# Scores of a lightning-attention layer from 96-row stacks of q and k halves, filled by transfers, instead of one zero-padded fp32 matmul a group

## The reference

```python
x = x + layernorm(attention(layernorm(x)))
x = x + layernorm(moe(layernorm(x)) + sigmoid(x @ shared_gate.T) * shared_ffn(layernorm(x)))

# attention: 16 heads of 32, chunks of 128 tokens, state S (32x32 a head) over a sequence
inter  = (q * decay_q) @ S
scores = (q @ k.T) * dmask            # 128 x 128 a head and chunk
intra  = scores @ v
S      = lam_c * S + (k * decay_k).T @ v
out    = inter + intra
```

## Time and profile before

| | |
|---|---|
| median of 3 runs | 1981.48 us (1980.39 to 1983.88) |
| the profiled execution | 1979.72 us, of which the span is 1977.9 |
| PE busy | 1883.4 us, 95% |
| DVE, ACT, POOL busy | 1084.6, 844.1, 437.3 us |
| transfers | 456.84 MB, 231 GB/s |

### The profile page before, as it was taken

How to read it: one execution, slowest core, us unless ns; L and a number is a source line. 1 busy time by engine, 2 the same in 40 slices (tenths; PEclk the granted TensorE clock), 3 DMA queues, 4 the chain that set the end, 5 groups by cost and what they waited for, 6 DMA issues and landing times.

```text
span 1977.9 us, 27565 instructions
## 1 busy us (share of the span) xinstructions
PE 1883.4 (95%) x9880; PEld 1530.1 (77%) x9880; DVE 1084.6 (55%) x2590; ACT 844.1 (43%) x1718; POOL 437.3 (22%) x438
## 2 busy tenths in 40 slices
PE   7779999999999998999999999989999999999997
PEld 5566777777777776777777777868899999999875
DVE  4556664564464463354464454353566667666566
ACT  4334443333343333333244233112566666666554
POOL 2301001001002000100100100120355656655322
PEclk9899999999999999999999999999999999999998
DMA  8978566646466446536556546687688999889597
GB/s 294 373 267 306 176 241 237 238 160 240 164 224 234 163 169 249 200 126 235 191 204 235 178 133 256 240 306 279 209 239 261 281 273 273 253 261 267 123 281 201
DMA packets 140869, 456.84 MB, mean 231 GB/s; under 512 B 17200, under 2 KB 17344, under 8 KB 123968
## 3 DMA queue, kind: packets, MB, share of 16 engines
q1 hardware_dynamic: 90720, 251.70, 36.3%
q0 software_dynamic: 49584, 203.33, 33.2%
q10 hardware_dynamic: 432, 0.07, 0.0%
HBM read 332.99 MB, written 122.04 MB: 230 GB/s over the span
## 4 chain that ended last, share of the span: by engine, by line
PE 63%; DVE 5%; DMA 1%; ACT 1%; issue 1%; SPq 0%; ACTq 0%; POOL 0%; DVEq 0%
PE banks L797 18%; PE banks L799 18%; PE banks L798 18%; PE banks L864 2%; PE banks L990 2%; PE banks L996 1%; PE banks L878 1%; PE banks L884 1%; PE banks L871 1%; DMA att_w_lo<-att_w_split 1%; PE banks L830 1%; DMA ffn_w_raw<-w_ffn 1%; DVE fin_stats L1536 0%; DVE probsT L1361 0%; PE banks L860 0%
## 5 line engine op out<-in xcount | busy, mean ns | idle before, releaser
L797 PE MATMUL banks<-xT_hi,ffn_gate_up_hi_lo 128*128 128x512 f32 x704 | 296.2, 421 | 10.1 <-DMA xT_lo<-xt_scratch 3.0
L799 PE MATMUL banks<-xT_hi,ffn_gate_up_hi_lo 128*128 128x512 f32 x704 | 276.2, 392 | 0.0
L798 PE MATMUL banks<-xT_lo,ffn_gate_up_hi_lo 128*128 128x512 f32 x704 | 275.1, 391 | 0.0
L797 PE MATMUL banks<-moe_gu_hi,moe_xT_hi 128*128 128x352 f32 x568 | 195.8, 345 | 0.3 <-DVE moe_xT_lo L1516 0.3
L1068 ACT COPY q_one_head<-qT 32x128 f32<-32x128 f32 x512 | 151.2, 295 | 88.6 <-PE banks L864 83.1
L799 PE MATMUL banks<-moe_gu_hi,moe_xT_lo 128*128 128x352 f32 x568 | 183.5, 323 | 0.0
L1509 DVE TENSOR_TENSOR moe_gu_lo<-moe_gu_raw,moe_gu_hi 128x704 fp32r<-128x704 f32 x156 | 136.3, 890 | 85.4 <-ACT moe_gu_hi L1129 77.0
L798 PE MATMUL banks<-moe_gu_lo,moe_xT_hi 128*128 128x352 f32 x568 | 182.4, 321 | 0.0
L797 PEld LDWEIGHTS banks<-xT_hi,ffn_gate_up_hi_lo 128*128 128x128 f32 x704 | 132.5, 188 | 50.2 <-issue 13.9
L683 POOL DMA_INDIRECT ffn_out<-moe_y,moe_x x71 | 123.6, 1741 | 159.0 <-DMA ffn_out<-moe_y,moe_x 40.6
L798 PEld LDWEIGHTS banks<-xT_lo,ffn_gate_up_hi_lo 128*128 128x128 f32 x704 | 132.7, 188 | 33.6 <-issue 8.9
(11 more groups left out here) (318 smaller groups left out, 4155.4 us busy)
## 6 DMA issues: line engine op xcount, KB each, us to landing
ffn_gate_up_hi_lo<-ffn_gate_up_split SPq DMA_DIRECT2D x66, 1024.0 KB
ffn_down_hi_lo<-ffn_down_split SPq DMA_DIRECT2D x66, 512.0 KB, 3.6
att_w_hi<-att_w_split SPq DMA_DIRECT2D x112, 256.0 KB, 4.0
att_w_lo<-att_w_split SPq DMA_DIRECT2D x112, 256.0 KB, 5.0
x_normed_by_expert<-x_normed POOLq DMA_DIRECT2D x26, 771.0 KB, 16.0
ffn_w_raw<-w_ffn SPq DMA_DIRECT2D x44, 384.0 KB, 6.3
ffn_gate_up_split<-ffn_gate_up_hi_lo SPq DMA_DIRECT2D x11, 1024.0 KB, 3.9
x_in<-x SPq DMA_DIRECT2D x32, 256.0 KB, 3.7
```

The source lines that it names most:

```text
L797: pe.matmul(out_ap, l_hi, r_hi, start=start, stop=False)
L798: pe.matmul(out_ap, l_hi, r_lo, start=False, stop=False)
L799: return pe.matmul(out_ap, l_lo, r_hi, start=False, stop=stop)
```

## The change

For blocks 1 to 7 the scores are made in another way. ACT copies q and k of a chunk, all four groups, rounded to fp32r (hi), and DVE subtracts them (lo): the new piece SQ, into `qk_parts`. SP then issues 12 transfers for each half of the groups, the new piece sx: for each of 4 heads of a group three 32-row bands, so that a stack of 96 rows holds q hi, q hi, q lo on one side and k hi, k lo, k hi on the other. The stacks lie in the memory of x_normedT (`qk_stack`). S is then four fp32r matmuls, 96 rows deep, 128 by 128, one for each head. Block 0 still has Z and the fp32 matmul. q_decayed now lies in qT itself for blocks 1 to 7. All the places of `PLACES` and `OPENING` are drawn anew, `PASSES` counts 2 for S, and in the expert stage the pieces XT and HT stand one place earlier.

```diff
 PLACES = {
...
-    "QK": (9.66, 11.07, 12.07, 13.22, 14.07, 15.07, 16.07, 16.78,),
+    "QK": (10.86, 11.47, 11.78, 11.8, 11.88, 12.85, 14.89, 15.52,),
...
+    "SQ": (17.03, 28.94, 33.88, 39.38,),
+    "sx": (23.79, 27.2, 27.41, 28.52, 33.14, 35.7, 42.92, 45.63,),
+    "KT": (25.54, 31.56, 37.12, 46.82,),
+    "S": (27.14, 27.84, 30.05, 30.38, 32.72, 33.54, 34.57, 35.31, 38.59, 39.3, 42.57, 43.12, 44.96, 47.22, 48.88, 49.38,),
...
@@ moe_step
-    split()
     if j + 1 < NJ:
         out += [("XT", j + 1)]
+    split()
+    if 1 <= j <= NJ:
+        out += [("HT", j - 1)]
     if live:
         out += [("GU", j, 1)]
     split()
-    if 1 <= j <= NJ:
-        out += [("HT", j - 1)]
...
+        xa = sb("x_normedT_hi_lo", [2, KT, TOK], F32R, scope=phase1)
+        xa_hi, xa_lo = xa[:, 0], xa[:, 1]
+        qk_stack = xa[:, :, :, :].rearrange("p s k t -> p (s k t)").rearrange("p (h s j g t) -> p h s j g t", h=2, s=2, j=GH, g=G // 2)
...
+        qk_parts = sb("qk_hi_lo", [2, 2, G, P], F32R, scope=phase1)
+        qz = qk_parts[:, 0].bitcast(F32)
...
+        def q_decayed(a, c):
+
+            return qT[:, :, c * P:(c + 1) * P] if a else first_qd
+
+        def stacked(a, c):
+
+            return 16 * 3 * GH * (NC * (a - 1) + c)
...
+            elif kind == "sx":
+                a, c, h = args
+                sp.wait_ge(v_piece, done("V", "SQ", a, c))
+                if c == 0:
+                    sp.wait_ge(p_piece, max(done("P", "V", a, NC - 1), done("P", "QK", a, 2 * G - 1)))
+                else:
+                    sp.wait_ge(p_piece, done("P", "S", a, c - 1, 2 * h + 1))
+                for r, (q_part, k_part) in enumerate(((0, 0), (0, 1), (1, 0))):
+                    for j in range(GH):
+                        src = qk_parts[j * HD:(j + 1) * HD, :, :, 2 * h:2 * h + 2, :].rearrange("p s i g t -> p (s i) (g t)")
+                        first, step = q_part, 2 + k_part - q_part
+                        sp.dma_start(out=qk_stack[r * HD:(r + 1) * HD, h, :, j].rearrange("p s g t -> p s (g t)").bitcast(F32),
+                                     in_=src[:, first:first + step + 1:step, :].bitcast(F32)).then_inc(stack_in[h], 16)
...
             elif kind == "S":
                 c, g = args
-                pe.wait_ge(a_piece, done("A", "Z", a, c, g))
-                mm = pe.matmul(b, kT[:, g, c * P:(c + 1) * P], qz[:, g % 2].rearrange("p h t -> p (h t)"),
-                               start=True, stop=True)
+                h, gl = divmod(g, 2)
+                pe.wait_ge(stack_in[h], stacked(a, c + 1))
+                for j in range(GH):
+                    mm = pe.matmul(b[:, j * P:(j + 1) * P], qk_stack[0:3 * HD, h, 1, j, gl, :], qk_stack[0:3 * HD, h, 0, j, gl, :],
+                                   start=True, stop=True)
...
+            elif kind == "SQ":
+                c, = args
+                if (a, c) == (1, 0):
+                    act.wait_ge(p_piece, done("P", "S", 0, NC - 1, G - 1))
+                if c == 0:
+                    act.wait_ge(a_piece, done("A", "QK", a, 2 * G - 1))
+                if (a, c) > (1, 0):
+                    for h in range(2):
+                        act.wait_ge(stack_in[h], stacked(a, c))
+                op = act.copy(qk_parts[:, :, 0], qkT[:, :, :, c * P:(c + 1) * P])
...
+                if a:
+                    ve.wait_ge(a_piece, done("A", "SQ", a, c))
+                    ve.wait_ge(v_piece, done("V", "SQ", a, c))
+                ve.tensor_tensor(q_decayed(a, c), qT[:, :, c * P:(c + 1) * P], dq[:, :, :], ALU.mult)
...
+            elif kind == "SQ":
+                c, = args
+                ve.wait_ge(a_piece, done("A", *piece))
+                op = ve.tensor_tensor(qk_parts[:, :, 1], qkT[:, :, :, c * P:(c + 1) * P], qk_parts[:, :, 0].bitcast(F32),
+                                      ALU.subtract)
```

More of the change, by code:

```diff
@@ L88 @@
[L88 to L110, removed]
+    "xin": (-26.98, -25.61, -25.39, -23.54,),
+    "N1A": (1.79,),
+    "N1B": (3.89,),
+    "N1": (4.54, 5.75, 7.57, 7.72,),
+    "T1": (5.87, 7.74, 8.2, 8.53,),
+    "wa": (5.47, 6.48, 8.73, 9.2, 11.13, 11.62, 12.83, 15.03, 14.9, 16.86, 17.56, 17.65, 25.58, 25.35, 23.26, 23.39,),
@@ new lines @@
+    "ST": (31.14, 36.38, 44.24, 53.74,),
+    "OUT": (32.88, 36.66, 44.63, 52,),
+    "LO": (37.13, 52.58,),
+    "LN": (40.01, 54.09,),
+    "L": (40.74, 55.29,),
+    "LX": (42.44, 56.85,),
+    "x1o": (40.59, 42.18, 54.75, 57.86,),
+    "T2": (43.87, 46.29, 59.01, 59.17,),
+    "xto": (61.05,),
+    "R1": (60.3,),
+    "R2": (63.97,),
+    "SM1": (64.06,),
+    "SM2": (64.16,),
+    "SM3": (64.51,),
+    "SM4": (66.38,),
+    "CM": (65.6,),
+    "RK": (68.51,),
+    "sc": (62.14,),
+    "PG": (69.92,),
@@ L122 @@
     "T1": (4.47, 5.52, 6.47, 6.59,),
[7 rows of a table removed]
-    "OUT": (28.96, 35.39, 44.8, 50.87,),
[9 rows of a table added]
+    "OUT": (29.04, 34.37, 46.23, 50.88,),
 }
-ARGS = {"Z": (NC, G), "S": (NC, G), "IP": (NC, 2)}
+ARGS = {"Z": (NC, G), "sx": (NC, 2), "S": (NC, G), "IP": (NC, 2)}
 def attention_offsets(a):
@@ L266, in final_chunk @@
     return [("FX", q), ("fo", q)]
-PASSES = {"T1": 2, "QK": 12, "V": 12, "KT": 2, "S": 4, "IP": 6, "ST": 4, "OUT": 12, "T2": 2, "R1": 12, "R2": 2, "RK": 1,
+PASSES = {"T1": 2, "QK": 12, "V": 12, "KT": 2, "S": 2, "IP": 6, "ST": 4, "OUT": 12, "T2": 2, "R1": 12, "R2": 2, "RK": 1,
           "GA": 12, "UP": 12, "DN": 12}
@@ L574, in build @@
         xt_used = sem("xT_used")
+        stack_in = [sem(f"qk_stack_in{h}") for h in range(2)]
         xs_zero, acc_zero, unused_id = sem("x1_by_expert_zero"), sem("ffn_out_zero"), sem("unused_row_id")
@@ L860, in pe_attention @@
                     mm = pe.transpose(b[:, g * P:(g + 1) * P], kT[:, g, c * P:(c + 1) * P], ident[:, :])
+            elif kind == "S" and a == 0:
+                c, g = args
+                pe.wait_ge(a_piece, done("A", "Z", a, c, g))
+                if c == 0:
+                    pe.wait_ge(a_piece, done("A", "QK", a, G + g))
+                mm = pe.matmul(b, kT[:, g, c * P:(c + 1) * P], qz[:, g % 2].rearrange("p h t -> p (h t)"),
+                               start=True, stop=True)
             elif kind == "S":
                 c, g = args
-                pe.wait_ge(a_piece, done("A", "Z", a, c, g))
-                mm = pe.matmul(b, kT[:, g, c * P:(c + 1) * P], qz[:, g % 2].rearrange("p h t -> p (h t)"),
-                               start=True, stop=True)
+                h, gl = divmod(g, 2)
+                pe.wait_ge(stack_in[h], stacked(a, c + 1))
+                for j in range(GH):
+                    mm = pe.matmul(b[:, j * P:(j + 1) * P], qk_stack[0:3 * HD, h, 1, j, gl, :], qk_stack[0:3 * HD, h, 0, j, gl, :],
+                                   start=True, stop=True)
             elif kind == "IP":
@@ L870, in pe_attention @@
                     g = 2 * half + gl
-                    pe.matmul(b[:, gl * P:(gl + 1) * P], state[:, g, :], qd[:, g, :], start=(gl == 0), stop=False,
+                    pe.matmul(b[:, gl * P:(gl + 1) * P], state[:, g, :], q_decayed(a, c)[:, g, :], start=(gl == 0), stop=False,
                               skip_group_check=True)
@@ L1018, in act_attention @@
                 c, = args
[L1019 to L1022 removed]
+                if kind == "T1" and a and c == 0:
+                    act.wait_ge(p_piece, done("P", "S", a - 1, NC - 1, G - 1) if a > 1 else
+                                max(done("P", "V", 0, NC - 1), done("P", "QK", 0, 2 * G - 1)))
+                if kind == "T2" and a > 1 and c == 0:
+                    act.wait_ge(p_piece, done("P", "R1", a - 1))
+                    act.wait_ge(xt_out, 32 * (a - 1))
                 op = act.copy((xa_hi if kind == "T1" else x1T(a)[0])[:, :, c * P:(c + 1) * P], chunked(b))
@@ L1600, in _ @@
             act.wait_ge(const_v, 7)
-            act.activation(qT[:, 0, 0:1], ones[:, 0:1], ACT.Identity, bias=ones[:, 0:1], scale=ones[:, 0:1])
+            act.activation(qkT[:, 0, 0, 0:1], ones[:, 0:1], ACT.Identity, bias=ones[:, 0:1], scale=ones[:, 0:1])
             for p in ORDER["A"]:
@@ L1626, in _ @@
                 ve.memset(t[:, :], 0.0).then_inc(const_v, 1)
-            late = next(p for p in ORDER["V"] if p[0] in ("V", "KT"))
+            late = next(p for p in ORDER["V"] if p[0] in ("V", "KT", "S"))
             for p in ORDER["V"]:
```

33 lines of the change are left out of this document (11 added, 22 removed), and 16 rows, old and new, of the table OPENING.

## The result

The changed kernel takes 2091.23 us (2085.55 to 2093.22, 4 runs), the kernel before 1981.12 on the same chip: ratio 1.0554 (95%: 1.0537 to 1.0570), 110 us slower, where 33 us faster was forecast. It is above the range of 1930 to 1996 by 95 us.

The account below looks back on a forecast made before the run. The prediction took TensorE (PE), busy 95% of the span, as the bound. From 1979.7 us, - 47 (matmul) + 13 (chain waits) + 5 (block 1) - 5 (kT) = 1945.7, about 1948 us on the median's scale; range 1930 to 1996.

Parts of the forecast that it names:

- Narrow matmul, 47 us off PE: Score pieces of blocks 1 to 7: 112 pieces at 0.44 us instead of 0.86, 47 us less.
- Issue 0.47 us, "5.6 us a group": SP's queue: transfers issue back to back every 0.47 us, so a group of 12 takes 5.6 us.
- The upper end of the range: Transfer chain's worst case: 67 us of PE waits, with landings of 5.0 us and each issue 0.05 us longer.
- Landing 2.4 us: Each group's transfers land 2.4 us after issue, the low end of 2.4 to 5.0 us seen.
- ACT's hi copy of the next chunk waits for this chunk's transfers ... so nothing is added: ACT's queue: the hidden_hi copy behind has slack and the score piece awaits the same transfers, so 0 us.
- The queue and its traffic, taken at nothing: SP's queue: DMA full only in bursts; the tightest FFN weight load, in block 3, holds by 2.4 us.
- PE waits about 3 us in four blocks and 0.3 in three: PE's waits for transfers in blocks 1 to 7: 13 us, plus 5 us for block 1's high DMA share.
- the sign of being wrong that the prediction named: PE's waits before the score pieces on DMA: some 18 us if right, over 50 us if wrong.
- KT moved, expert stage, block 0: The 5.2 us wait for kT goes (-5); expert stage 0, still without idle; block 0 taken as 0, +-8 us.
- narrow fp32r costing as fp32: Rival: a score piece takes 0.89 us for 0.86, no gain, 1988 us; chance 0.13.
- the hidden chain: Rival: short landings and longer PE parts hide the transfer chain, no 13 us of waits, 1935 us; chance 0.13.
- The chain in the place of the matmul's time: Rival: before first score pieces of chunks 0 and 1, PE waits 67 us for 18, 1997 us; chance 0.16.

Follow-up runs that it names:

- experiments 5 and 7: Changed kernel with all transfers' rows cut to 64 bytes, 2054.64 us; or with half as many transfers, of 128 KB, on SP alone, 2243.37 us.
- experiment 4: Changed kernel, transfers reading a constant tile so ACT's copies wait for no landing: 2053.73 us; PE not waiting either: 2015.78 us; that with 64-byte rows: 1997.58 us.
- experiment 3: Changed kernel with all transfers and the waits of ACT and SP, but score matmuls read a spare tile, so PE does not wait for transfers: 2085.19 us.
- experiment 5: Changed kernel with 4 of the 12 transfers of each group: 1981.46 us; with all transfers, rows cut from 1 KB to 64 bytes: 2054.64 us.

## Why the prediction was wrong, by its own steps

- *Narrow matmul, 47 us off PE:* the size was right (46 us of busy time, 0.44 us a piece), the worth was not. Without any transfer it is worth 27 us, since 14 us come back as idle time, 6 of them as waits for probsT.
- *Issue 0.47 us, "5.6 us a group":* it measured 0.60, 0.64 with the gap, 7.6 to 8.8 us a group. The earlier trace rows are loads of weights, and no row of the kernel before has a transfer of this form. What makes its issue longer stays open: it is not the bytes (experiments 5 and 7) and not the step in the source, which the constant source of experiment 4 has not, at the same 597 ns. The upper end of the range allowed 0.05 more, not 0.17. In block 3 the first stack was in at 13.9 us behind V (forecast 9.9), the second at 28.0 (18.2), the third at 40.5 (28.6).
- *Landing 2.4 us:* 1.5 (552.3 to 553.87, the third group), 3.9 (523.3 to 527.2, the first) and 5.0 (536.2 to 541.25, the second, in a full queue): within the 5.0 of the upper end.
- *"ACT's hi copy of the next chunk waits for this chunk's transfers ... so nothing is added":* **this is the first of two steps that failed.** It looked at one instruction behind the copy and at one engine. Behind it stand hidden_hi and attT_hi, and on DVE the lo subtraction and the masks. This wait alone, with PE's own taken away, makes the loss whole (experiment 3), 69 us of it due to the wait. Without it 31 of the 134 us go (experiment 4).
- *The queue and its traffic, taken at nothing* (the FFN weights hold by 2.4 us, bursts only): **this is the second.** With nobody waiting for a transfer the kernel takes 2016 us (experiment 4), already above the 1996 of the range. 66 us of it are the transfers: 47 us with transfers of 4 KB, and 19 for the rest of their bytes, 29 in the changed kernel (experiment 5). The waits that show it are mostly for x transposed, whose loads I did not place at all, and not for FFN weights.
- *"PE waits about 3 us in four blocks and 0.3 in three", with the 5 added 18 us, 67 at most:* the direct waits were 69.6 us, which is the sign of being wrong that the prediction named. They are worth 37 us where ACT does not wait, and nothing on top where it does.
- *Clock:* not priced. 46 of the 134 us are the same PE instructions at the lower level.
- *KT moved, expert stage, block 0:* the wait for kT went; 1500 to 1940 us is busy for 439.5 of 440; 0 to 60 us has 46.3 us of busy time against 45.4. These three held.
- *Rivals:* narrow fp32r costing as fp32 was wrong, the hidden chain too. The chain in the place of the matmul's time was the right direction with the wrong size, 1997 for 2091: it counted PE's direct waits and let each delay count once. My reading of the rest, which no run takes apart further: the loop closes several times a block, and a stall of PE delays the pieces that free buffers for SP, so that SP's next group starts later.

## What to carry to other kernels

When a copy must wait for its reader's transfers to land, price the wait by everything queued behind it on that engine and on those that wait for it, not by its own consumer alone. Place every other load of the same queue as well: here the transfers cost 66 us with nobody waiting for them. Count the whole loop (copy, issues, landing, copy) against the work between two rounds before counting any single wait, and add the slower clock behind each stall of PE. A row "PE <- DMA" names who came last: taking PE's wait away here changed nothing, while taking away the wait on a mostly idle engine gave back 31 us of 134.
